# The last attention head of a graph network: its second weight chunk in the other slot, its activations finished third by third

## The reference, cut to what matters

```python
h = (x @ W1).reshape(n, H1, D)                 # H1 = 8 heads of D = 768
e = leaky_relu(alpha_src[src] + alpha_dst[dst])
alpha = softmax of e over the edges of each dst  # a 256 x 256 matrix for each head
out = segment_sum(h[src] * alpha, dst) + b1
hid = elu(out)                                 # 256 x (8 * 768)
out2 = gat_conv(hid, W2, one head)             # hid @ W2, then attention again
x = x + out2 + b2
```

## Time and profile before

| | us |
|---|---|
| median of three runs | 1469.46 |
| the profiled execution | 1471.03 |
| its span, first to last instruction | 1469.0 |
| TensorE busy with matmuls | 1300.3 (89%) |
| VectorE busy | 1003.7 (68%) |
| ScalarE busy | 625.4 (43%) |
| granted TensorE clock, mean | 0.93 |

### The profile page before, as it was taken

One profiled execution on the slowest core, in us unless ns is written; L12 is line 12 of the kernel. 1 busy time (PEld: TensorE's weight loads), 2 busy tenths in 40 slices (PEclk: granted clock), 3 DMA queues, 4 the chain that ended last, 5 costly groups with the idle time before them and its releaser, 6 DMA issues.

```text
span 1469.0 us, 20882 instructions
## 1 busy us (share of the span) xinstructions
PE 1300.3 (89%) x7595; PEld 1165.7 (79%) x7598; DVE 1003.7 (68%) x1663; ACT 625.4 (43%) x786; POOL 220.4 (15%) x160
## 2 busy tenths in 40 slices
PE   5599999956699999966678799999999999999886
PEld 3499999854589999965567698888988988988775
DVE  7888888767587888854854665665656656656544
ACT  2256655445255665543423433434334334333411
POOL 0034444320024444430000000000000000002000
PEclk9899999986789999986878899999999999999977
DMA  9465565542256556533323344454453543544600
GB/s 346 129 198 180 164 199 180 179 119 87 73 171 208 168 164 201 178 107 108 113 78 142 114 184 165 147 205 148 163 194 143 182 175 143 199 150 148 200 17 22
DMA packets 103716, 227.29 MB, mean 155 GB/s; under 512 B 16688, under 2 KB 34672, under 8 KB 103684
## 3 DMA queue, kind: packets, MB, share of 16 engines
q1 hardware_dynamic: 74940, 196.37, 37.9%
q10 hardware_dynamic: 18808, 27.85, 6.4%
q0 software_dynamic: 9936, 2.66, 2.0%
HBM read 216.56 MB, written 10.29 MB: 154 GB/s over the span
## 4 chain that ended last, share of the span: by engine, by line
PE 66%; DVE 20%; issue 7%; ACT 4%; DMA 1%; DVEq 0%; SPq 0%; ACTq 0%
PE bank L411 64%; DVE w_lo L1097 5%; DVE h_lo L1097 1%; DVE hid_lo L1097 1%; ACT w_hi L831 1%; DVE scores_b L1185 1%; DVE neg_b L1237 1%; DVE scores_b L1187 1%; PE bank L445 1%; PE bank L496 1%; DVE scores_b L1103 1%; DVE alpha L1100 1%; DMA w_in<-ffn_in 1%; DVE neg_b L1100 1%; DVE stats L1125 1%
## 5 line engine op out<-in xcount | busy, mean ns | idle before, releaser
L1097 DVE TENSOR_TENSOR w_lo<-w_in,w_hi 128x2304 fp32r<-128x2304 f32 (+4 forms) x162 | 396.3, 2477 | 87.1 <-ACT w_hi L831 87.0
L831 ACT ACTIVATE w_hi<-w_in 128x2304 fp32r<-128x2304 f32 (+4 forms) x162 | 327.9, 2062 | 240.7 <-PE bank L411 204.4
L411 PE MATMUL bank<-w_hi,xT_hi 128*128 128x384 f32 (+3 forms) x942 | 326.9, 347 | 12.0 <-DVE w_lo L1097 6.1
L411 PE MATMUL bank<-w_hi,hid_hi 128*128 128x512 f32 (+2 forms) x858 | 298.8, 348 | 26.0 <-DVE hid_lo L1097 21.9
L411 PE MATMUL bank<-w_lo,xT_hi 128*128 128x384 f32 (+3 forms) x942 | 312.4, 344 | 0.0
L411 PE MATMUL bank<-w_lo,hid_hi 128*128 128x512 f32 (+2 forms) x858 | 276.6, 343 | 0.0
L411 PE MATMUL bank<-w_hi,xT_lo 128*128 128x384 f32 (+3 forms) x942 | 249.0, 343 | 0.0
L411 PE MATMUL bank<-w_hi,hid_lo 128*128 128x512 f32 (+2 forms) x858 | 228.4, 343 | 0.0
L411 PEld LDWEIGHTS bank<-w_hi,hid_hi 128*128 128x128 f32 (+1 forms) x858 | 166.0, 193 | 62.6 <-DVE hid_lo L1097 21.7
L411 PEld LDWEIGHTS bank<-w_hi,xT_hi 128*128 128x128 f32 (+1 forms) x942 | 180.6, 192 | 40.1 <-issue 9.1
L411 PEld LDWEIGHTS bank<-w_lo,xT_hi 128*128 128x128 f32 (+1 forms) x942 | 180.7, 192 | 14.4 <-issue 1.1
(11 more groups left out here) (226 smaller groups left out, 1497.7 us busy)
## 6 DMA issues: line engine op xcount, KB each, us to landing
w_in<-L_gnn_W_rel SPq DMA_DIRECT2D x68, 1152.0 KB, 5.5
w_in<-L_gnn_W SPq DMA_DIRECT2D x66, 1152.0 KB, 5.6
table<-zrow SPq DMA_DIRECT2D x1, 9216.0 KB, 36.9
scores_b<-table ACTq DMA_DIRECT2D x34, 256.0 KB, 2.9
a_bc<-L_gnn_a_src ACTq DMA_DIRECT2D x18, 384.0 KB, 3.7
a_bc<-L_gnn_a_dst ACTq DMA_DIRECT2D x18, 384.0 KB, 4.8
key_row<-key_rows SPq DMA_DIRECT2D x15, 256.0 KB, 3.3
w_in<-ffn_out SPq DMA_DIRECT2D x4, 864.0 KB, 6.7
```

Of the source, the lines that this page charges most:

```text
L411: return pe.matmul(out, lhsT, rhs, start=start, stop=stop, **kw)
L831: act.activation(out, ps, func, **kw).then_inc(mark, 1)
L1097: return dve.tensor_tensor(out, a, b, op)
```

## The change

In the last head of both layers W2 goes to the slot of W1 (free once `up` of head 7 is over), so its two halves are rounded where the other heads round the next W1: the first half ahead of the softmax's exponentials, the second behind alpha's rounding. The six steps from z to hid are interleaved by thirds in the last head. `down_last` waits for the first third, does all four output tiles over feature tiles 0 and 1, then waits for the other two thirds and does feature tiles 2 to 5. What follows W2 (FFN0, FFN1) goes to the other slot, and layer 1 has all its slots swapped (W1 in slot 1, W2 in slot 0). Cut to its core:

```diff
+        def half_of(c):
+            return (c + 1) % 2 if c in (C_FFN0, C_FFN0 + 1) else c % 2
 # TensorE: up reads slot `layer` instead of 0, down reads slot 1 - layer instead of 1
                 def down_last(h, n):
+                    weights(n)
                     for j in range(3):
                         pe.wait_ge(hid_low, (h + HEADS * layer) * 3 + j + 1)
-                    weights(n)
-                    for m, (b, c0_, c1, o) in SUMMED:
-                        for k in range(K):
-                            last = mm3([(bank[b][:, c0_:c1], of_w(1)(k, o, o + c1 - c0_))],
...
+                        if j == 1:
+                            continue
+                        for m, (b, c0_, c1, o) in SUMMED:
+                            for k in ((0, 1) if j == 0 else (2, 3, 4, 5)):
+                                last = mm3([(bank[b][:, c0_:c1], of_w(layer)(k, o, o + c1 - c0_))],
...
+                            if j == 0:
+                                continue
 # ScalarE, in head()
-                    if not last_head:
-                        high(h * 2 + (n0 + 2), h * 2 + (c0 + 3), 0, parts=(0,))
+                    high(h * 2 + (n0 + 2), h * 2 + (c0 + 3), layer, parts=(0,))
                     attend(u, ahead)
-                    if not last_head:
-                        high(h * 2 + (n0 + 2), h * 2 + (c0 + 3), 0, parts=(1,))
-                    n2 = n0 + 2 * HEADS if last_head else h * 2 + (n0 + 3)
-                    if last_head:
-                        high(n2, h * 2 + (c0 + 4), 1)
+                    high(h * 2 + (n0 + 2), h * 2 + (c0 + 3), layer, parts=(1,))
...
+                    if last_head:
+                        kept(0)
+                        kept(1)
+                        exponential(0)
+                        kept(2)
+                        exponential(1)
+                        rounded(0)
+                        exponential(2)
+                        rounded(1)
+                        rounded(2)
+                        high(nth(c0 + 18), c0 + 18, 1 - layer, SHAPES[c0 + 18])
 # VectorE, in head()
-                    scores(h + 9 * layer, layer, lambda: None if last_head else low(h * 2 + (n0 + 2), 0, parts=(0,)))
-                    if last_head:
-                        low(n0 + 2 * HEADS, 1)
-                    else:
-                        low(h * 2 + (n0 + 2), 0, parts=(1,))
+                    scores(h + 9 * layer, layer, lambda: low(h * 2 + (n0 + 2), layer, parts=(0,)))
+                    low(h * 2 + (n0 + 2), layer, parts=(1,))
...
                     if last_head:
+                        negative(0)
+                        negative(1)
+                        unit(0)
+                        negative(2)
+                        unit(1)
+                        remainder(0)
+                        unit(2)
+                        remainder(1)
+                        remainder(2)
                         batch_firsts(b)
```

More of the change, by code:

```diff
@@ L519, in up @@
                                 pair(ln_low, 6 * layer, k)
-                            last = mm3([(bank[banks[j]][:, 0:HALF], part(w_hi, w_lo, slice(0, P), 0, k, slice(j * HALF, (j + 1) * HALF)))
+                            last = mm3([(bank[banks[j]][:, 0:HALF], part(w_hi, w_lo, slice(0, P), layer, k, slice(j * HALF, (j + 1) * HALF)))
                                         for j in range(2)],
@@ L533, in down @@
                             pe.wait_ge(w_low[k // 3], n + 1)
-                        last = mm3([(bank[b][:, c0_:c1], of_w(1)(k, o, o + c1 - c0_)) for (b, c0_, c1, o) in SUM_BANKS[m]],
+                        last = mm3([(bank[b][:, c0_:c1], of_w(1 - layer)(k, o, o + c1 - c0_)) for (b, c0_, c1, o) in SUM_BANKS[m]],
                                    part(hid_hi, hid_lo, slice(0, P), k, slice(m * P, (m + 1) * P)), False,
@@ L540, in down_last @@
                 def down_last(h, n):
+                    weights(n)
                     for j in range(3):
                         pe.wait_ge(hid_low, (h + HEADS * layer) * 3 + j + 1)
-                    weights(n)
-                    for m, (b, c0_, c1, o) in SUMMED:
-                        for k in range(K):
-                            last = mm3([(bank[b][:, c0_:c1], of_w(1)(k, o, o + c1 - c0_))],
[L548 to L553, removed]
+                        if j == 1:
[3 more added lines that the diff above has]
+                                last = mm3([(bank[b][:, c0_:c1], of_w(layer)(k, o, o + c1 - c0_))],
+                                           part(hid_hi, hid_lo, slice(0, P), k, slice(m * P, (m + 1) * P)), False,
+                                           k == K - 1, skip_group_check=True)
+                            if j == 0:
+                                continue
+                            if b == 1:
+                                last.then_inc(w_used, 2)
+                            elif (b, m) != (2, 0):
+                                last.then_inc(sum_mm, 1)
                 def attend(h):
@@ L628, in _ @@
             for k in range(K):
-                last = mm3([(bank[4][0:FH, 0:N], part(xT_hi, xT_lo, slice(0, P), k))], of_w(0)(k, 0, FH), k == 0, k == K - 1)
+                last = mm3([(bank[4][0:FH, 0:N], part(xT_hi, xT_lo, slice(0, P), k))], of_w(1)(k, 0, FH), k == 0, k == K - 1)
             last.then_inc(w_used, 1)
@@ L893, in head, with kept @@
-                    if last_head:
-                        high(n2, h * 2 + (c0 + 4), 1)
+                    high(h * 2 + (n0 + 2), h * 2 + (c0 + 3), layer, parts=(1,))
                     a = (h + HEADS * layer) * 3
-                    for j, b in enumerate((5, 3, 4)):
+                    def kept(j):
                         act.wait_ge(att_mm, a + (j + 1))
                         for k in (2 * j, 2 * j + 1):
-                            last = act.activation(z_b[:, k, :], bank[b][:, (k % 2) * N:(k % 2 + 1) * N], ACT.Identity,
+                            last = act.activation(z_b[:, k, :], bank[(5, 3, 4)[j]][:, (k % 2) * N:(k % 2 + 1) * N], ACT.Identity,
@@ L900, in head, with exponential, rounded @@
                                                   bias=b1_head[:, k:k + 1])
                         last.then_inc(z_kept, 1)
-                    for j in range(3):
+                    def exponential(j):
                         act.wait_ge(z_neg, a + (j + 1))
                         keep(neg_b[:, 2 * j:2 * j + 2, :], neg_b[:, 2 * j:2 * j + 2, :], z_exp, ACT.Exp)
-                    for j in range(3):
+                    def rounded(j):
                         act.wait_ge(elu, a + (j + 1))
@@ L907, in head @@
                         keep(hid_hi[:, 2 * j:2 * j + 2, :], neg_b[:, 2 * j:2 * j + 2, :], hid_high)
-                    if not last_head:
-                        high(n2, h * 2 + (c0 + 4), 1)
+                    if last_head:
[9 more added lines that the diff above has]
+                        high(nth(c0 + 18), c0 + 18, 1 - layer, SHAPES[c0 + 18])
+                    else:
+                        for stage in (kept, exponential, rounded):
+                            for j in range(3):
+                                stage(j)
+                        high(h * 2 + (n0 + 3), h * 2 + (c0 + 4), 1 - layer)
@@ L1117, in low_chunk @@
             def low_chunk(c, parts=(0, 1)):
-                low(nth(c), c % 2, SHAPES.get(c, WHOLE), parts)
+                low(nth(c), half_of(c), SHAPES.get(c, WHOLE), parts)
             moments_taken = [0]
@@ L1238, in head, with remainder @@
                                                  flat(z_b[:, 2 * j:2 * j + 2, :]), add_, mx).then_inc(elu, 1)
-                    if not last_head:
-                        batch_firsts(b)
-                    for j in range(3):
+                    def remainder(j):
                         dve.wait_ge(hid_high, a + (j + 1))
@@ L1244, in head @@
                     if last_head:
+                        negative(0)
[7 more added lines that the diff above has]
+                        remainder(2)
                         batch_firsts(b)
                     else:
-                        low(h * 2 + (n0 + 3), 1)
+                        for stage in (negative, unit):
+                            for j in range(3):
+                                stage(j)
+                        batch_firsts(b)
+                        for j in range(3):
+                            remainder(j)
+                        low(h * 2 + (n0 + 3), 1 - layer)
                 head(0, first_head=True)
```

17 lines of the change are left out of this document (8 added, 9 removed).

## The result

| | us |
|---|---|
| before, median of 10 runs | 1469.88 |
| changed, median of 10 runs | 1460.14 (1456.45 to 1463.70) |
| ratio | 0.9932, 95% interval 0.9919 to 0.9945 |
| span of the profiled execution, before and changed | 1469.0 and 1459.6 |

The change makes the kernel faster by 0.68%, about 10 us (8.1 to 11.9). The forecast was 8.5 us, 1461.0, in a range of 1456.5 to 1465.5.

The account below looks back on a forecast made before the run. TensorE's stretches, joined by short pieces where it stands still, were taken to bound the kernel. Layer 1's 5.5 us plus layer 0's 3.0 us made 8.5 us, from the median 1469.46 to 1461.0; range 1456.5 to 1465.5.

Parts of the forecast that it names:

- the walk of the queues: Last head, ScalarE and VectorE steps by thirds: `down_last` starts at 637.93 instead of 642.84, 4.9 us earlier.
- the FFN0 load: Layer 0's last head: this load ends last; released earlier through `batch_firsts`, it and the dots move by 3.0 us.
- the rival on the clock: Layer 1's `down_last`: no slow clock after the 2.9 us wait, 10.1 us gained in all, 1459.4; chance 0.15.
- W2's move at no cost: Last head: W2's rounding and remainders fit where head 6 has the next W1's, with 2.4 and 1.7 us of cover.
- rival of slow handovers: Last heads: each of 12 ScalarE-VectorE handovers costs 0.2 us more, 2.4 us lost per layer, 1465.8; chance 0.12.
- The split: `down_last` in two parts: 24 of 72 matmuls keep TensorE busy over 4 us, so no second wait; last dots unharmed.
- Layer 1's 5.5 us: Layer 1's last head: 4.9 us from the earlier `down_last` plus 0.6 us from the clock.
- the forecast's case: Layer 1's `down_last`: clock at 0.50 for 3.2 us after the wait, 1.6 us lost instead of 2.2.
- The table loads: ScalarE, last heads: rival that six function changes each load a table at 1.28 us, 4.9 us slower, 1474.4; chance 0.03.
- prediction's aside: ScalarE table loads: at the skill page's about 2.7 us per switch, the loss would be twice the rival's 4.9 us.
- The rest of the time: Stages behind the two last heads: costed at nothing, with 1 us each way for the clock.

Follow-up runs that it names:

- W2 late: Changed kernel, but the last head rounds both halves of W2 only after head 6's `down`, ahead of the six steps: 1466.16 us, ratio 0.9978 against before.
- second execution of the kernel before: The kernel before the change, run once more without any edit: 1468.66 us.
- first profile: For the changed kernel, its first profiled execution, without further edits: span 1459.6 us.
- second repetition: The changed kernel profiled a third time, without any edit: 1461.04 us.
- first repetition: The changed kernel profiled a second time, without any edit: 1462.32 us.
- W2 alone: Against the kernel before, only W2's move to the other slot, without interleaving or split `down_last`: 1461.46 us, ratio 0.9950.
- layer 1 alone: Changed kernel, but layer 0's last head has W2 rounded late, no interleaving and no split: 1461.90 us, ratio 0.9933 against before.
- the last: Changed kernel plus FFN0's load ahead of the counting row's and 12 idle matmuls in the wait before `down_last`: 1451.62 us, ratio 0.9872 against before.

## Why the prediction was right

The time lies in the range and the two mechanisms, the walk of the queues and the FFN0 load, came out as told. The size is partly luck: at the marks the three profiles of the changed kernel give 9.8, 7.0 and 8.5 us, 8.4 on average, against 8.5 forecast; the whole time moved by 10, nearer to the 10.1 of the rival on the clock, and the rest lies outside the two stages.

- **W2's move at no cost:** right. In layer 1 ScalarE's first half of W2 ended 2.2 us ahead of the exponentials (2.4 in head 6 before), in layer 0 it was 1.9 us, and in layer 1 `aT_lo` was ready 1.7 us before `attend` began. The experiment with W2 late shows that all the rest hangs on it.
- **The walk of the two queues:** right to 0.1 us: `down_last` at 7.34 us after `attend` began, against 637.93 - 630.51 = 7.42. One small slip in it does no harm: by its own terms the first exponential ends at 634.99 and not 635.05. Such walks, made after this profile was seen (the 9.3 starts from its last remainder), gave 9.9, 8.7, 9.3 and 11.2 us for four other orders; measured were 9.75, 8.55, 9.34 and 11.11. The rival of slow handovers is out with it: on the chain VectorE goes on 0.02 us after ScalarE.
- **The split:** right, there is no second wait of TensorE inside `down_last`, and layer 1's last dots wait only for the last tile.
- **Layer 0 bound by the FFN0 load:** right, 2.7 us of 3.0. The load itself took 8.67 us instead of 8.40, the missing 0.3; that is scatter, for in the second execution of the kernel before it took 8.79 and the mark was at 28.23, 3.1 us later than in the changed kernel. `batch_firsts` began 9.1 us after `attend` (9.2 forecast). That it stands behind the counting row is shown by the experiment that swaps the two.
- **Layer 1's 5.5 us:** 7.1 in the first profile, 5.7 on average over three. The term that was too simple is the clock: I took one value (0.6 us of gain) for what is a draw. The rival "the clock does not fall", which had a chance of 0.15, came true in the first profile, the forecast's case (3.2 us slow) in the second repetition with 3 us slow, and in the first repetition a longer fall, which loses 0.7 us against before (15.6 instead of 14.9 us).
- **The table loads:** none. The rule in the Trainium skill, "ScalarE: Activation LUTs", section "Rules for kernel authors", is about switches between sets; here the six changes of function cost nothing (ScalarE's rows above follow each other by 0.5 us, 0.7 behind a z of two instructions). The prediction's aside that by the page's figure the loss would be twice its own is a wrong sum. Four and six loads of 2.7 us, less the 4.9 and 3.0 us gained, leave about 19 us of loss, four times as much; this is an estimate from the page's figure, while the load in the earlier trace rows took 1.28 us.
- **The rest of the time.** The two stages explain 7.0 to 9.8 us in the three profiles; 8.1 to 11.9 were measured. The forecast costed the clock of the other stages at nothing, with 1 us each way; the last section shows that it moves by 3 us and more.

## What to carry to other kernels

When a wait behind a handed-over tile is long, list what stands in the two queues ahead of it that the tile doesn't need: here 5 us of weight preparation had to leave before interleaving and splitting could bring anything. Look for the load that ends last in each stage by itself, and for what stands ahead of it in its queue; moving one line of SyncE's queue gave 2.9 us. Judge such a change at a mark inside the stage, in the profile, because the clock elsewhere moves the whole time by some 3 us, as much as the smaller variants gain. When the sum of several stages comes out as expected, check each one too.

## What the runs showed of the hardware

The same wait of TensorE, 2.87 us, was followed by anything from 0 to 6 us at 1.2 GHz, at the same place: of the nine cases (both layers in four profiles, one in a fifth) three were fast throughout. After 7.79 to 7.89 us the clock was slow at first in all five cases, and so it was in the eight after the waits of 4.07 to 6.64 us in the variants. With matmuls of zeros in the wait (12 issued, 11 in the records) the clock was 1.00 afterwards in all four cases, both layers of two kernels.

This is also where the whole time spreads. In a stage that no kernel here changes, near the end, the same 43 instructions of VectorE and the matmuls between them took 43.9 us in the first profile of the kernel before and 40.9 in the second, at a mean clock of 0.74 and 0.79. The window of the first profile:

```profile
1410.10:1454.00 43.90, 37.85 (x179) 33.65 (x180) 15.94 (x43) 9.10 (x11) 0.00 (x0) 0.74 0.00 0
```

The second profile:

```profile
1410.70:1451.60 40.90, 34.85 (x177) 30.74 (x177) 15.90 (x43) 9.08 (x11) 0.00 (x0) 0.79 0.00 0
```

The gains in the whole time lie above those at the marks in most of the kernels (7.4 against 5.1 for W2 alone, 3.2 against -0.4 for W2 late, 9.9 against 3.8 for layer 1 alone, 18.8 against 14.2 for the last), though below in one (5.4 against 5.9). For W2 late the record says where the difference lies. The windows of the stretch behind layer 1's mark, with the same 4294 matmuls, in the kernel before and with W2 late:

```profile
658.48:1469.00 810.52, 737.31 (x4294) 654.98 (x4294) 479.71 (x596) 293.26 (x294) 12.30 (x11) 0.92 0.40 142
660.14:1464.50 804.36, 729.16 (x4294) 647.62 (x4294) 479.33 (x596) 293.39 (x294) 13.32 (x11) 0.93 0.41 143
```

VectorE and ScalarE did the same work in the same time; TensorE was busy some 8 us less, and the stretch was 6.2 us shorter (2.8 us against the second execution of the kernel before, whose stretch took 807.1). It holds beyond single executions, since each has its mean granted clock on record. The span times (1 - clock) is an estimate of what the slow clock costs: on average 99.3 us in the 19 executions of the kernel before and 96.1 in the 12 with W2 late. What is left of the span is 1368.4 and 1368.5 us. By this estimate the whole gain of W2 late lies in the clock and none of it in shorter waits. In the same way most of the scatter between the 19 executions of the kernel before is the clock's: their standard deviation is 2.6 us, and 1.0 with the estimate taken off.

What stays open is why the later stages, whose work is the same, get more of the fast clock in one kernel than in another.
